# A graph network kernel: POOL paces its indirect transfers by their landing, with one semaphore per pair

## What is computed

```
x = layernorm(x + net0(x, edges))     # 4 rounds over all edges, see below
x = layernorm(x + attention(x, edge_attr_64, edge_attr_9, edges))
x = layernorm(x + net2(x, edge_attr_16, edges))
x = layernorm(x + convolution(x, edges))

net0, one round:                       # row = src, col = dst
    m   = silu(concat(h[row], h[col]) @ w1 + b1)
    m   = silu(m @ w2 + b2)
    agg = segment_sum(m, row)
    h   = h + silu(concat(h, agg) @ m1 + c1) @ m2 + c2
attention:                             # keys and values from x[dst], query from x[src]
    k, v = tensor_product(x[dst], edge_sh, mlp(edge_features))
    out  = segment_softmax over src of (q[src] . k), times v, summed by src
net2:        silu(silu(concat(x[src], x[dst], edge_attr) @ W1 + b1) @ W2 + b2), summed by dst
convolution: sum by dst of x[src] / sqrt(deg[src] * deg[dst])
```

## Time and profile before

| | us |
|---|---|
| median of three runs | 14986.72 |
| lowest and highest | 14971.17, 15014.58 |
| profiled execution, its own time | 14971.03 |
| its span in the profile | 14969.2 |
| PE busy, share of the span | 8661.8 (58%) |
| POOL busy | 7753.7 (52%) |
| DVE busy | 5960.0 (40%) |
| ACT busy | 2260.3 (15%) |

### The profile page before, as it was taken

One profiled execution on the slowest core, in us unless ns is written; L12 is line 12 of the kernel. 1 busy time (PEld: TensorE's weight loads), 2 busy tenths in 40 slices (PEclk: granted clock), 3 DMA queues, 4 the chain that ended last, 5 costly groups with the idle time before them and its releaser, 6 DMA issues. The chain is left out here.

```text
span 14969.2 us, 187510 instructions
## 1 busy us (share of the span) xinstructions
PE 8661.8 (58%) x45093; PEld 7113.9 (48%) x45094; DVE 5960.0 (40%) x14867; ACT 2260.3 (15%) x3991; POOL 7753.7 (52%) x7547
## 2 busy tenths in 40 slices
PE   2004778774555555555555555899995656664333
PEld 1004654444445444544444444688884545554222
DVE  4115730002333233323333333588888833333222
ACT  0000023330000100010001000355552000000000
POOL 5661025555555555545554555345452445554666
PEclk9999987776767667766766676799997867776555
DMA  1002333332111311121111111488884311111111
GB/s 24 1 1 65 107 120 118 113 109 52 37 38 36 62 37 38 37 59 37 39 38 47 38 36 38 139 249 250 249 250 122 114 37 42 42 41 29 22 22 22
DMA packets 853397, 1107.22 MB, mean 74 GB/s; under 512 B 336740, under 2 KB 530569, under 8 KB 852295
## 3 DMA queue, kind: packets, MB, share of 16 engines
q1 hardware_dynamic: 304698, 470.90, 11.2%
q0 software_dynamic: 264160, 418.34, 10.4%
q10 hardware_dynamic: 284332, 215.58, 5.6%
HBM read 896.28 MB, written 207.86 MB: 74 GB/s over the span
## 5 line engine op out<-in xcount | busy, mean ns | idle before, releaser
L1190 POOL DMA_INDIRECT gx_l<-xr,gi_l x4160 | 4226.8, 1016 | 3461.8 <-DVE gi_l L1277 2256.1
L1299 DVE TENSOR_TENSOR aggT_l<-aggT_l,psum 64x128 f32 x4160 | 1160.8, 279 | 4072.3 <-remote 2102.0
L1827 PE MATMUL psum<-cw,xa 128*128 128x256 f32 x6656 | 1517.3, 382 | 37.5 <-issue 31.0
L935 POOL DMA_INDIRECT slots_d<-eo,row_d x806 | 787.3, 977 | 1375.7 <-ACT eo L1081 1098.1
L1815 POOL DMA_INDIRECT gx<-xr,gi x832 | 893.5, 1074 | 1042.7 <-DVEq L1903 687.0
L1827 PEld LDWEIGHTS psum<-cw,xa 128*128 128x128 f32 x6656 | 1232.9, 190 | 260.4 <-issue 108.7
L1229 PE MATMUL psum<-b,onesb 3*128 3x512 bf16 x520 | 259.6, 499 | 1835.3 <-ACT h_l L1256 1466.5
L1354 PE MATMUL psum<-ptab,oht 128*128 x6656 | 989.8, 300 | 550.0 <-issue 493.3
L1354 PEld LDWEIGHTS psum<-ptab,oht 128*128 128x128 f32 x6656 | 929.0, 217 | 593.5 <-issue 592.5
L2406 POOL DMA_INDIRECT gx_l<-xr,gi_l x832 | 828.1, 995 | 497.2 <-issue 231.0
L1883 ACT COPY xT<-psum 32x512 f32<-32x512 f32 x1664 | 957.5, 575 | 606.7 <-remote 480.3
(11 more groups left out here) (361 smaller groups left out, 13404.3 us busy)
## 6 DMA issues: line engine op xcount, KB each, us to landing
wkv<-slots_d ACTq DMA_DIRECT2D x208, 568.0 KB
kr<-keyrow_s SPq DMA_DIRECT2D x416, 256.0 KB
shb<-shT SPq DMA_DIRECT2D x1664, 64.0 KB
gx_l<-xr,gi_l POOLq DMA_INDIRECT x4992
vtab<-kv ACTq DMA_DIRECT2D x208, 256.0 KB
v_in<-vtab SPq DMA_DIRECT2D x104, 512.0 KB, 3.6
hT<-noderow SPq DMA_DIRECT2D x101, 512.0 KB
kr<-keyrow_d SPq DMA_DIRECT2D x208, 128.0 KB
```

The lines of the kernel that those rows point to most:

```text
L935: e_gone[j].at(pool.indirect_dma_start(slots["d"], bass.IndirectOffsetOnAxis(ap=row["d"][:, c0 + t:c0 + t + 1], axis=0), eo[j][:, t, :], N ...
L1190: pool.indirect_dma_start(gx[j][:, c_, :], None, xr, bass.IndirectOffsetOnAxis(ap=gi[j][:, c_:c_ + 1], axis=0), engine_sem=described.sem). ...
L1299: ins = dve.tensor_tensor(a, a, sums(j, h), ALU.add)
L1827: ins = pe.matmul(bank[2 + p][:, t % 2 * OKV:(t % 2 + 1) * OKV], xa[j][:, c, t * P:(t + 1) * P], cw[:, c, :], start=c == 0, stop=c == KC - 1)
```

## The change

The semaphore `described` is gone, and with it its increment by every transfer. POOL now starts each pair of indirect transfers when the pair two back has landed. For that each buffer of rows has one semaphore per pair in place of one for all: `rows_in[j][h]` with h from 0 to 3 (0 and 1 in the logits), `e_gone[j][h]`, and `scattered[j]` with j the pair's number modulo 3. The wait comes also to L935, which had none, and takes the place of the wait per block of 13 in L920. Whoever waits for a whole buffer of rows waits for all its pairs: DVE at L1311, PE in the logits and in the convolution, SP where a table is read back. Two waits of DVE ahead of the copy of the row numbers change: in a net pass it is dropped, and in the convolution it is a wait for PE's sums of the item four back. No other instruction is added, removed or moved.

```
-LEAD = 2
+PAIR = 2
@@ scatter_s_pool
-                j = c // SC % 2
+                j = c // PAIR % 3
...
-                if c % SC == 0 and c >= 2 * SC:
-                    pool.wait_ge(scattered[j].sem, scattered[j].n)
-                    pool.nop(nofuse=True)
-                if c >= 2 * LEAD and c % LEAD == 0:
-                    pool.wait_ge(described.sem, described.n - LEAD)
+                if c >= 2 * PAIR and c % PAIR == 0:
+                    two_back = scattered[(c // PAIR - 2) % 3]
+                    pool.wait_ge(two_back.sem, two_back.n)
                     pool.nop(nofuse=True)
@@ scatter_d_pool
                 for t in range(i * EW - c0, EW):
-                    e_gone[j].at(pool.indirect_dma_start(
+                    if i and t % PAIR == 0:
+                        two_back = e_gone[(i - 1) % AHEAD][t // PAIR]
+                        pool.wait_ge(two_back.sem, two_back.n)
+                        pool.nop(nofuse=True)
+                    e_gone[j][t // PAIR].at(pool.indirect_dma_start(
@@ rows_gone
-            eng.wait_ge(e_gone[i % AHEAD].sem, 16 * EW * (i // AHEAD + 1))
+            for h in range(EW // PAIR):
+                eng.wait_ge(e_gone[i % AHEAD][h].sem, 16 * PAIR * (i // AHEAD + 1))
@@ messages_pool, and conv_pool with rows_in3
-                            if c_ % LEAD == 0 and (c_ or k.has(0, 1)):
-                                pool.wait_ge(described.sem, described.n + i * W + (c_ - LEAD))
+                            h = c_ // PAIR
+                            if c_ % PAIR == 0 and (h >= 2 or k.has(0, 1)):
+                                s_, two_back = (0, rows_in[j][h - 2]) if h >= 2 else (1, rows_in[k.buf(1, AHEAD)][h + 2])
+                                pool.wait_ge(two_back.sem, two_back.n + k.uses(s_, AHEAD) * (16 * PAIR))
                                 pool.nop(nofuse=True)
-                            pool.indirect_dma_start(gx[j][:, c_, :], None, xr, bass.IndirectOffsetOnAxis(ap=gi[j][:, c_:c_ + 1], axis=0),
-                                                    engine_sem=described.sem).then_inc(rows_in[j].sem, 16)
+                            pool.indirect_dma_start(gx[j][:, c_, :], None, xr,
+                                                    bass.IndirectOffsetOnAxis(ap=gi[j][:, c_:c_ + 1], axis=0)).then_inc(rows_in[j][h].sem, 16)
@@ messages_dve
-                        if k.has(0, AHEAD):
-                            dve.wait_ge(rows_in[j].sem, rows_in[j].n + (k.uses(0, AHEAD) - 1) * (16 * W))
...
-                        dve.wait_ge(rows_in[r].sem, rows_in[r].n + k.uses(3, AHEAD) * (16 * W))
+                        for h in range(W // PAIR):
+                            dve.wait_ge(rows_in[r][h].sem, rows_in[r][h].n + k.uses(3, AHEAD) * (16 * PAIR))
@@ logits_pool
-                        if t % LEAD == 0 and (t or k.has(0, 1)):
-                            pool.wait_ge(described.sem, described.n + i * GT + (t - LEAD))
+                        h = t // PAIR
+                        if t % PAIR == 0 and k.has(0, 1):
+                            two_back = rows_in1[k.buf(1, AHEAD)][h]
+                            pool.wait_ge(two_back.sem, two_back.n + k.uses(1, AHEAD) * (16 * PAIR))
@@ conv_pe
-                    pe.wait_ge(rows_in3[j].sem, rows_in3[j].n + k.uses(3, AHEAD) * (16 * W))
+                    for h in range(W // PAIR):
+                        pe.wait_ge(rows_in3[j][h].sem, rows_in3[j][h].n + k.uses(3, AHEAD) * (16 * PAIR))
@@ conv_dve
-                        dve.wait_ge(rows_in3[j].sem, rows_in3[j].n + (k.uses(0, AHEAD) - 1) * (16 * W))
+                        dve.wait_ge(summed.sem, summed.n + i - (AHEAD - 1))
```

More of the change, by code:

```diff
@@ L146, in build @@
         loaded = sig("loaded")
-        described = sig("described")
         def join():
@@ L892, in first_column @@
             return min(i * EW, EC - EW)
-        scattered = [sig(f"scattered{j}") for j in range(2)]
+        scattered = [sig(f"scattered{j}") for j in range(3)]
         feats_in = [sig(f"feats_in{j}") for j in range(2)]
@@ L897, in build @@
         rec_in = sig("rec_in")
-        e_gone = [sig(f"e_gone{j}") for j in range(AHEAD)]
+        e_gone = [[sig(f"e_gone{j}_{h}") for h in range(EW // PAIR)] for j in range(AHEAD)]
         def group_dmas(g):
@@ L981, in table_s_sp @@
         def table_s_sp():
-            for j in range(2):
+            for j in range(3):
                 sp.wait_ge(scattered[j].sem, scattered[j].n)
@@ L1155, in edge_messages @@
             keys_in = [sig(f"keys_in{j}") for j in range(2)]
-            rows_in = [sig(f"rows_in{j}") for j in range(AHEAD)]
+            rows_in = [[sig(f"rows_in{j}_{h}") for h in range(W // PAIR)] for j in range(AHEAD)]
             feat_in = [sig(f"feat_in{j}") for j in range(2)]
@@ L1330, in edge_messages @@
             part_added.n += n * (ng - 1)
-            described.n += n * W
             if feature:
@@ L1335, in edge_messages @@
             for j in range(AHEAD):
-                rows_in[j].n += 16 * W * len(range(j, n, AHEAD))
+                for h in range(W // PAIR):
+                    rows_in[j][h].n += 16 * PAIR * len(range(j, n, AHEAD))
             for j in range(2):
@@ L1603, in scatters_end @@
             for j in range(AHEAD):
-                sp.wait_ge(e_gone[j].sem, e_gone[j].n)
+                for h in range(EW // PAIR):
+                    sp.wait_ge(e_gone[j][h].sem, e_gone[j][h].n)
             sp.nop(nofuse=True)
@@ L1775, in build @@
         keys_in1 = [sig(f"keys_in{j}") for j in range(2)]
-        rows_in1 = [sig(f"rows_in{j}") for j in range(AHEAD)]
+        rows_in1 = [[sig(f"rows_in{j}_{h}") for h in range(GT // PAIR)] for j in range(AHEAD)]
         wrows_in = [sig(f"wrows_in{j}") for j in range(2)]
@@ L1846, in turn @@
                     i, j, r = k.i(1), k.buf(1), k.buf(1, AHEAD)
-                    pe.wait_ge(rows_in1[r].sem, rows_in1[r].n + k.uses(1, AHEAD) * (16 * GT))
+                    for h in range(GT // PAIR):
+                        pe.wait_ge(rows_in1[r][h].sem, rows_in1[r][h].n + k.uses(1, AHEAD) * (16 * PAIR))
                     upto(pe, "xT_set", k, 1, 1)
@@ L1920, in turn @@
                         r = k.buf(2, AHEAD)
-                        dve.wait_ge(rows_in1[r].sem, rows_in1[r].n + k.uses(2, AHEAD) * (16 * GT))
+                        for h in range(GT // PAIR):
+                            dve.wait_ge(rows_in1[r][h].sem, rows_in1[r][h].n + k.uses(2, AHEAD) * (16 * PAIR))
                     dve.tensor_copy(gi1[j][:], gidx["d"][:, bass.ds(i * GT, GT)]).then_inc(s1["gi1_set"].sem, 1)
@@ L1957, in build @@
             s1[x].n += G
-        described.n += G * GT
         for j in range(AHEAD):
-            rows_in1[j].n += 16 * GT * (G // AHEAD)
+            for h in range(GT // PAIR):
+                rows_in1[j][h].n += 16 * PAIR * (G // AHEAD)
         for j in range(2):
@@ L2391, in build @@
         tile_added = sig("part_added")
-        rows_in3 = [sig(f"rows_in{j}") for j in range(AHEAD)]
+        rows_in3 = [[sig(f"rows_in{j}_{h}") for h in range(W // PAIR)] for j in range(AHEAD)]
         def conv_pool():
@@ L2402, in turn @@
                     for c_ in range(W):
-                        if c_ % LEAD == 0 and (c_ or k.has(0, 1)):
-                            pool.wait_ge(described.sem, described.n + i * W + (c_ - LEAD))
+                        h = c_ // PAIR
+                        if c_ % PAIR == 0 and (h >= 2 or k.has(0, 1)):
+                            s_, two_back = (0, rows_in3[j][h - 2]) if h >= 2 else (1, rows_in3[k.buf(1, AHEAD)][h + 2])
+                            pool.wait_ge(two_back.sem, two_back.n + k.uses(s_, AHEAD) * (16 * PAIR))
                             pool.nop(nofuse=True)
-                        pool.indirect_dma_start(gx[j][:, c_, :], None, xr, bass.IndirectOffsetOnAxis(ap=gi[j][:, c_:c_ + 1], axis=0),
-                                                engine_sem=described.sem).then_inc(rows_in3[j].sem, 16)
+                        pool.indirect_dma_start(gx[j][:, c_, :], None, xr,
+                                                bass.IndirectOffsetOnAxis(ap=gi[j][:, c_:c_ + 1], axis=0)).then_inc(rows_in3[j][h].sem, 16)
             turns(pool, n3, 4, 6, turn, AHEAD)
@@ L2460, in build @@
         for j in range(AHEAD):
-            rows_in3[j].n += 16 * W * len(range(j, n3, AHEAD))
+            for h in range(W // PAIR):
+                rows_in3[j][h].n += 16 * PAIR * len(range(j, n3, AHEAD))
         join()
```

7 lines of the change are left out of this document (3 added, 4 removed).

## The result

The changed kernel takes 14,807.7 us (median of 4 runs, 14,791.1 to 14,811.7), beside 14,993.3 us (14,971.2 to 15,014.6) for the kernel before: a ratio of 0.9875, 95% interval 0.9862 to 0.9888. It is 186 us faster; the forecast was 15,010 us, no change. The profiled execution has a span of 14,802.3 us, 167 less than before.

A forecast was written before the change was run, and what follows sets the result against it. POOL's 7436 indirect transfers shape the stages, with late signals the largest loss. Profiled 14,971 us plus 26 for waits is 14,997, plus 16 to the median 15,013, rounded 15,010 us; forecast range 14,930 to 15,070, whole range 14,150 to 15,400.

The forecast's parts named there:

- The reading of late signals: Whole kernel: while POOL runs without pause other engines' signals arrive late, ACT's first silu waiting 13.5 us each; pauses release them.
- The wait that the change replaces: POOL's wait on descriptions two pairs back: passed in time, gathers 1.25 us apart with 0.30 us gaps; exchanging it costs nothing.
- relief rival: Late signals ease through fewer transfers handed ahead or no count; 14,240 us at a quarter, 14,700 at a tenth; chance 0.31.
- The landing gate's margin of 0.31 us: Net passes and last convolution: landing plus start 2.49 us against 2.80 us of cover, so the new gate costs nothing.
- no idle time put down to its own landings beyond the 193 us: POOL's gathers: sign that the gate costs nothing, its landing idle time staying at 193 us and 33 us.
- that rival: Late gate: landing passes 1.83 us and POOL pauses before pairs; 0.1 us on 2496 pairs, +250 us, 15,260; chance 0.20.
- The 2.08 us for a landing: Gathers: counted from POOL's span end, makes 3.05 us against 2.80, +620 us on 2496 pairs; not adopted, 1.52 us was.
- Second scatter and first scatter: New landing gate in the slots_d scatter and the source scatter: each taken at 0, upper ends 133 and 121 us.
- Logits at 0: Logits gathers: landing 4.28 us plus start 0.97 us against 6.4 us of cover, so nothing except in the first turns.
- More waits for DVE and PE, 26 us: Readers wait for one semaphore per pair: 0.1 us once in two turns, 26 us; upper end 104 us.
- The convolution's new order at 0: Convolution: index copy waits for PE's sums of four turns back, but POOL already waits for that count; nothing.
- three signs for relief: ACT's silu waits well below 13.5 us, a net pass under 1400 us, sorting ended before the first scatter.

The follow-up runs named there:

- e4: Changed kernel, but in the five net passes each turn's first pair waits until the pair just before it has landed; ratio 0.9469 where signals are late.
- e1: Changed kernel with the gate on descriptions and the count per transfer put back, rest of the change kept; ratio 1.0021 where signals are late.
- e2: Changed kernel with no gate on pairs in any stage and no count per transfer; ratio 0.9900 where signals are late.
- e3: Changed kernel with its landing gate, the count of descriptions still raised by transfers except in slots_d; ratio 0.9917 where signals are late.
- e5: Changed kernel with description waits and count put back in the five net passes only, landing gate elsewhere; ratio 1.0125 where signals are prompt.
- f4: Changed kernel with no gate on pairs and no count, the kernel of e2, where signals are prompt; ratio 1.0032.
- g1: Kernel before with a description wait per transfer, twice the waits and fewer transfers handed ahead; ratio 1.0073 where signals are late.
- f1: The changed kernel itself, run where signals are prompt; ratio 1.0239 to the kernel before.
- g5: Changed kernel with a stop on landing every eight transfers in first scatter, net passes and convolution; 13,518 us, ratio 0.9218 where signals are late.
- g3: Changed kernel with landing gate in the net passes only, description waits in first scatter, logits and convolution, none in second scatter; ratio 0.9888, late signals.
- g4: Changed kernel with each landing gate one pair looser, on the pair three back; ratio 0.9930 where signals are late.
- e8: The kernel of g5, with the same stops on landing, run where signals are prompt; ratio 1.1681 to the kernel before.

## Why the prediction was wrong, step by step

**The reading of late signals** holds. They are the largest loss, POOL's pauses let them through (e4), and the sorting behind the first scatter and POOL's waits for indices are what can be had, as the rival had listed. Its "all of it", 3088 us less (2256 of waits for indices, 832 of sorting), was near: between the two kinds lie 3,200 to 3,600 us, and the 11,900 us that it didn't believe are what the kernel takes, and less, where signals are prompt.

**The wait that the change replaces, valued at nothing: this step failed.** The argument was that both gates are passed in time, so that exchanging them changes nothing. For POOL that is nearly true. For the others it isn't: the wait on descriptions, with its count, costs 1.2% where signals are late (e1 against e2; 1.0% of it with the count kept, e3) and nothing where they are prompt (e5's passes against f4's). The prediction looked only at POOL's own gaps in the earlier trace rows. Its relief rival had the right sign at 0.31, but offered two reasons: fewer transfers handed ahead (falls: e2 has more ahead and gains, g1 has fewer and loses) and no count raised per transfer (not the main part: e3 keeps most of the gain with it). The third reason, the wait itself, wasn't on the list, and the size was too large: 186 us against 310 for a tenth.

**The landing gate's margin of 0.31 us** was right in the typical case and too simple as a whole. It was worked out from single landings; some come later. Where signals are late that shows as 1.71 us in one gap and 80 us more of idle time in all; that POOL would otherwise have spent it on waiting for indices is my reading. The sign "no idle time put down to its own landings beyond the 193 us" took 632 ordinary gaps at the old gate for landings. Where signals are prompt the gate is late in the sense of that rival, but that its 250 us are close to the 237 measured is luck: on its 2496 pairs (passes and convolution) f1 loses 135 us to f4, 0.05 us each, and 93 us come from the two scatters, which it didn't count. The 2.08 us for a landing, an estimate that the prediction worked out from the Trainium skill (DMA: Bandwidth & Descriptors, "Anatomy of one DMA — SWDGE (gpsimd) path"), would have made it 620 us on the same pairs. The prediction counted it from the end of POOL's span. f1 against f4 has 135 us there, and in f1 landings come 1.46 us behind that end in the median and 2.4 us behind its start, so the traces don't bear that way of counting out.

**Second scatter and first scatter, taken at 0** with 133 and 121 us as upper ends: 45 and 47 us without late signals (f1 against f4), 28 us gained and 8 us lost with them. **Logits at 0**: 1781 against 1787 us, right for the stage. The reason given, a gate with 6.4 us of cover that stops nobody, is not what f1 shows: landings there come 5.1 us behind the span in the median, where one row had 4.28, and POOL waits 275.8 us in 84 gaps for them. It waits 251 us less for DVE in return (381.8, f4 632.7), and the stage takes 1759 us in both. **More waits for DVE and PE, 26 us**: e1 (1.0021, 23 us between the medians) and f4 (1.0032, 36 us) contain them with the other small edits; right in size, though nothing shows them alone. **The convolution's new order at 0**: 1225 against 1227 us, right. **What would show it** had three signs for relief: ACT's waits well below 13.5 us (they are at 12.2), a pass under 1400 us (1403 to 1424), sorting ended before the first scatter (no). The relief that came is a small part of what they were written for; the signs as written would have been met by e4 and g5.

**Open**: why a wait of POOL on descriptions delays the signals of others (only its effect is shown); whether the two-back gate's small pauses add 0.4% (g3 against g4); what makes a chip late or prompt. Not run: the kernel before without its waits on descriptions and nothing else changed; half the waits where signals are late; the changed kernel in a second late group.

## What to carry to other kernels

A wait that never stops its own engine can still cost the other engines: an exchange of one wait for another is not free because the gaps are the same, and its price is found by taking it out (e2), not from the trace of before. If a trace shows waits on "remote" that end just after POOL stops, try one stop of POOL per turn before any finer work: two microseconds every eight transfers took 5% off here in the net passes alone and 8% with the first scatter and the convolution, where signals were late. Measure such an edit several times and on several chips, since the same stops cost 17%, and the landing gate 2.4%, where signals came promptly. Of the versions tried in both kinds, no gate on pairs at all is the best compromise, 0.990 and 1.003; a landing gate three pairs back has 0.993 and 1.007. Whether a kernel with more transfers in hand can go without a gate wasn't tried.

## What the runs showed of the hardware

- One and the same kernel takes 14,600 to 15,000 us in some groups of runs and 11,380 to 11,400 in others, each steady within 0.7%; the difference goes with signals between PE, DVE and ACT that arrive late (in the trace before the change 13.5 us on the average for ACT's first silu, 19.2 at the longest) while POOL issues indirect transfers without pause, and it is gone from every stage in which POOL stops every eight transfers (g5 against e8). This was not expected at all.
- With a stop of 2.1 us every 12.5 us the late waits are gone but for two; with a stop of 1.0 us that only waits for descriptions ACT's fall from 13.5 us in the trace before the change to 9.0 us.
- POOL's waiting on the count of its own descriptions costs the other engines 1.0 to 1.2% of the time where signals are late; raising the count costs 0.4% at most (e3 against the changed kernel, from two groups).
- A gather's landing is 1.46 us behind POOL's span in the median, but 27 of 1248 come later than the 1.83 us that the gate has to spare, the last 10.9 us behind. The gates on landings together cost 2% when POOL is the bound, the scatters' among them.
